# The causal mask of an attention stage put into the score banks by ScalarE copies, where TensorE products with an identity put it before

## The reference, cut to what matters

```python
x = x + _L0_xattn_ref(_layernorm(x, axis=-1), ctx_512, L0_xattn_Wq, L0_xattn_Wkv_expand, L0_xattn_Wout)
...
scores = jnp.einsum('bhqd,bhkd->bhqk', qh, kh) * inv_sqrt_d
causal = jnp.tril(jnp.ones((sq, sk), dtype=bool))
scores = jnp.where(causal, scores, jnp.finfo(scores.dtype).min)
attn = jax.nn.softmax(scores, axis=-1)
out = jnp.einsum('bhqk,bhkd->bhqd', attn, vh)
```

## Time and profile before

| what | value |
|---|---|
| median of 3 runs | 667.65 us (663.9 to 668.47) |
| the profiled execution: its time, its span | 663.85 us, 662.3 us |
| TensorE busy over the span | 593.4 us (90%) |
| VectorE, ScalarE, GpSimd busy | 406.2 us (61%), 294.2 us (44%), 161.9 us (24%) |
| mean granted TensorE clock | 0.957 of full |
| attention stage | 0 to about 143 us of the span |

### The profile page before, as it was taken

The page is one execution under the profiler, slowest core; times in us unless marked ns, Lnnn a source line. Parts: engine busy times, 40 slices in busy tenths (PEclk is TensorE's granted clock), DMA queues, the critical chain, the costliest instruction groups (busy, mean ns, idle before and its releaser), DMA issues.

```text
span 662.3 us, 10646 instructions
## 1 busy us (share of the span) xinstructions
PE 593.4 (90%) x3622; PEld 468.4 (71%) x3642; DVE 406.2 (61%) x790; ACT 294.2 (44%) x477; POOL 161.9 (24%) x245
## 2 busy tenths in 40 slices
PE   4887999765888758699999999999999999999995
PEld 3666877562555436488888888888888888888884
DVE  5766778757999844656766555555555555555553
ACT  3477666433998843534444332333323322333232
POOL 6434495927676744000000000000000000000000
PEclk9899999767999976999999999999999999999999
DMA  9500000020000031445545113111231222241121
GB/s 254 183 2 1 2 2 2 1 64 2 1 1 1 1 127 51 115 108 148 139 118 140 52 68 124 64 64 64 64 127 63 63 63 65 79 109 63 64 63 47
DMA packets 37465, 45.91 MB, mean 69 GB/s; under 512 B 10720, under 2 KB 24688, under 8 KB 37296
## 3 DMA queue, kind: packets, MB, share of 16 engines
q1 hardware_dynamic: 34304, 41.19, 20.8%
q0 software_dynamic: 1008, 3.67, 1.7%
q10 hardware_dynamic: 2112, 0.52, 0.4%
HBM read 41.04 MB, written 4.33 MB: 68 GB/s over the span
## 4 chain that ended last, share of the span: by engine, by line
PE 60%; ACT 1%; POOL 1%; DVE 1%; issue 1%; DVEq 0%; POOLq 0%
PE psY L1341 6%; PE psG L1328 6%; PE psY L1344 6%; PE psY L1343 6%; PE psG L1329 6%; PE psG L1330 6%; PE psU L1328 6%; PE psU L1330 6%; PE psU L1329 6%; PE psAux L1269 1%; PE psT L1269 1%; PE psY L1289 1%; PE psT L1354 1%; POOL r_rstd L1235 1%; ACT gw L1455 0%
## 5 line engine op out<-in xcount | busy, mean ns | idle before, releaser
L1427 ACT ACTIVATE act_hi<-x_tok 128x512 fp32r<-128x512 f32 x88 | 55.7, 633 | 161.9 <-DVE x_tok L1556 161.9
L1549 DVE TENSOR_TENSOR x_tok<-psU,x_tok 128x512 f32<-128x512 f32 x88 | 60.8, 692 | 103.1 <-PE psU L1330 100.6
L1560 DVE TENSOR_TENSOR act_lo<-x_tok,act_hi 128x512 fp32r<-128x512 f32 x88 | 60.8, 692 | 62.6 <-ACT act_hi L1427 62.5
L1421 ACT ACTIVATE x_tok<-psG 128x512 f32<-128x512 f32 x88 | 52.7, 601 | 58.0 <-PE psG L1330 58.0
L1246 POOL DMA_DIRECT2D out_dram<-x_tok x3 | 2.3, 773 | 300.8 <-DVE x_tok L1567 300.8
L1341 PE MATMUL psY<-act_hi,wd_lo 128*128 128x512 f32 x176 | 71.0, 404 | 5.0 <-DVE act_lo L1560 5.0
L1328 PE MATMUL psG<-h3T_hi,wg_lo 128*128 (+1 forms) x176 | 69.9, 397 | 0.3 <-DVE logit L1593 0.3
L1344 PE MATMUL psY<-act_hi,wd_hi 128*128 128x512 f32 x176 | 69.2, 393 | 0.0
L1343 PE MATMUL psY<-act_lo,wd_hi 128*128 128x512 f32 x176 | 69.1, 392 | 0.0
L1329 PE MATMUL psG<-h3T_lo,wg_hi 128*128 (+1 forms) x176 | 69.0, 392 | 0.0
L1330 PE MATMUL psG<-h3T_hi,wg_hi 128*128 (+1 forms) x176 | 69.0, 392 | 0.0
(11 more groups left out here) (223 smaller groups left out, 1160.5 us busy)
## 6 DMA issues: line engine op xcount, KB each, us to landing
cw_rows<-cw_spill SPq DMA_DIRECT2D x80, 128.0 KB, 2.9
cw_rows<-cw_spill SPq DMA_DIRECT2D x16, 224.0 KB, 2.9
cw_rows<-cw_spill SPq DMA_DIRECT2D x16, 192.0 KB, 2.7
w_stage<-in_L_ffn_w_gate_dram SPq DMA_DIRECT2D x11, 256.0 KB, 2.9
w_stage<-in_L_ffn_w_up_dram SPq DMA_DIRECT2D x11, 256.0 KB, 2.8
cw_rows<-cw_spill SPq DMA_DIRECT2D x16, 160.0 KB, 2.5
wg_nat<-in_L_attn_w_gate_dram SPq DMA_DIRECT2D x1, 2048.0 KB, 16.3
x_spill<-x_tok SPq DMA_DIRECT2D x1, 2048.0 KB, 7.3
```

The source lines that it names most:

```text
L1421: nc.scalar.activation(a[s % 2][:, :], psG[s % 2][:, :], ACT.Silu).then_inc(s_silu, 1)
L1427: nc.scalar.activation(a_hi[s % 2][:, :], a[s % 2][:, :], ACT.Copy).then_inc(s_ahi, 1)
L1549: nc.vector.tensor_tensor(a[s % 2][:, :], psU[s % 2][:, :], a[s % 2][:, :], ALU.mult).then_inc(s_t, 1)
L1560: nc.vector.tensor_tensor(a_lo[s % 2][:, :], a[s % 2][:, :], a_hi[s % 2][:, :].bitcast(F32), ALU.subtract).then_inc(s_alo, 1)
```

## The change

ScalarE gets a new step `masked(j, u)`: a copy of the mask from SBUF (bf16) into the score bank u % 2, as soon as VectorE has taken the shifted scores of step u out of it. TensorE's two mask products stay for the very first half (pair 0, half 0) only; the other halves wait for the count of the copies instead (`s_masked`). The wait for `s_sub` stays in place. The last pair needs no copies behind its steps 2 and 3.

```diff
+        s_masked = b.sem("a_masked")
...
+                def masked(j, u):
+
+                    need(act, s_sub, 4 * j + u + 1)
+                    nc.scalar.activation(psS[u % 2][:, :], k.causal[:, :, :].rearrange("p h s -> p (h s)"), ACT.Copy
+                                         ).then_inc(s_masked, 1)
...
                     if two:
                         exps(i - 1, 0)
+                        masked(i - 1, 0)
                     if three:
                         probs_out(i - 2, 2)
                         probs_out(i - 2, 3)
                     if two:
+                        masked(i - 1, 1)
                         exps(i - 1, 1)
...
                         exps(i - 1, 2)
+                        if i < NP:
+                            masked(i - 1, 2)
+                            masked(i - 1, 3)
                         exps(i - 1, 3)
...
-                    for r in range(2):
-                        nc.tensor.matmul(psS[r][:, :], k.identb[:, :],
-                                         k.causal[:, :, :].rearrange("p h s -> p (h s)"), start=True, stop=True,
-                                         skip_group_check=True)
+                    if j == 0 and t == 0:
+                        for r in range(2):
+                            nc.tensor.matmul(psS[r][:, :], k.identb[:, :],
+                                             k.causal[:, :, :].rearrange("p h s -> p (h s)"), start=True, stop=True,
+                                             skip_group_check=True)
+                    need(pe, s_masked, 4 * j + 2 * t)
```

## The result

The changed kernel takes 672.2 us (median of 7 runs, 670.81 to 675.67) against 667.65 (7 runs, 663.9 to 669.64): a ratio of 1.0083, 95% interval 1.005 to 1.0116. It is slower by 0.8%, near the forecast of 671, and inside the 1% that was called hard to tell. Its profiled execution took 673.75 us with a span of 672.2, 9.9 more than the one before. That is twice the difference of the medians, and the last experiment says why.

A forecast was written before the change was run, and what follows sets the result against it. The prediction took a loop over TensorE, VectorE and ScalarE in the attention stage as the bound. Copies and removed products summed to 14c - 8m = 6.72 - 3.52 = +3.2 us on 667.65, forecast 671, range 662 to 680.

The forecast's parts named there:

- The loop: Attention stage: path over TensorE, VectorE and ScalarE said to set the pace, 13.54 us a plain turn.
- plain turns: Attention turns between 4 and 7, without weight sums: said to grow from 13.54 to about 14.06 us.
- The term c: Time of one ScalarE mask copy from SBUF to PSUM: taken as 0.48 us, 0.54 as other end.
- The term m: Time of one pair of TensorE mask products taken away: 0.44 to 0.53 us, taken as 0.44.
- TensorE's reserve: TensorE's 0.34 us wait ahead of attend 2: removing the 7 first-half pairs was said only to lengthen it.
- c - m: Turn 1 to 2: one copy added, one pair of products removed; the copy ahead of exponential 3 hides.
- 3c - m: Turns 2 to 3 and 3 to 4, with weight sums: three copies added, one pair of products removed, each.
- 2c - m: Turns 4 to 5, 5 to 6 and 6 to 7: two copies added, one pair of products removed, each.
- c - 2m: Turn 7 to 8: input scales hide one copy, one stays; the removed pair counts twice at halved clock.
- The wait of attend 2: TensorE's wait for pT ahead of attend 2: from 0.34 to 1.7 us in plain turns, some 1.9 in turn 3.
- The clock rival: Longer TensorE waits ahead of attend 2 drop its clock again and again: 675 to 680 us, chance 0.25.
- one more drop at most: Condition of the main forecast: loop grows, TensorE's clock drops at most once more; 667 to 675 us, chance 0.52.

The follow-up runs named there:

- the last experiment: Kernel before, unedited, profiled and timed once more: ratio 1.002, profiled span 666.3 us against 662.3.
- with the wait filled: Changed kernel with TensorE doing the products of the queries twice in turns 2 to 7: 667.49 us, ratio 1.0029 against the kernel before.
- products gone: Kernel before without TensorE's 30 mask products and with no copies, mask left out behind the first half: 659.26 us, ratio 0.9913.

## Why the prediction was right

**The loop** of the plain turns was read rightly in each step: it runs from the scores over VectorE, ScalarE's last exponential, `pT` copies and `hT_hi`, VectorE again, exponential 0 and `pT` to attend 2. Moving one copy by two places, or dropping two of the four, changed the turn by one step each. Four turn lengths that were on record before their runs, 14.6, 13.10, 14.13 and 13.61, were met within 0.02 us (the 14.13 had been read in the changed kernel's profile). VectorE's wait for `hT_hi` grew from 0.38 to 0.88 us, the 0.5 that was forecast.

**The term c** (0.48, with 0.54 as its other end) was a little low: 0.52 ahead of `pT`, 0.54 ahead of exponential 3. With 0.53 the sum is 14 x 0.53 - 3.52 = +3.9 instead of +3.2. A plain turn was said to be 14.06 and is 14.13. That ScalarE reaches PSUM faster than SBUF, as the Trainium skill has it in "ScalarE: Activation LUTs" ("Step-by-step: what each stage is for"), holds but is small: the copy takes 592 ns on average into the banks and 622 into the spare tile.

**The term m** was taken as 0.44 and is 0.44 (2.67 to 2.23). The 0.09 us ahead of the scores' smaller weights stayed. That first halves lie in TensorE's reserve was shown by the run without the products.

**What was hidden and what was not**: the copies of steps 1 and 2 in plain turns cost nothing, as predicted. Outside the plain turns three terms were off. Second half to second half, with no slow stretch in between except in turn 8, where both kernels have it:

| interval | forecast | measured | from |
|---|---|---|---|
| 1 to 2 | c - m = +0.04 | +0.47 | 13.82 to 14.29, changed kernel |
| 2 to 3 | 3c - m = +1.0 | +1.02 | 15.47 to 16.49, with the wait filled |
| each plain turn | 2c - m = +0.52 | +0.59 | 13.54 to 14.13 |
| 7 to 8 | c - 2m = -0.4 | -1.15 | 15.22 to 14.07, changed kernel |

In turn 1 to 2 the row statistics covered less than half of the copy ahead of exponential 3: `hT_lo` had no wait before, and now waits 0.30 us and starts 0.34 later.

```profile
31.40 0.69 DVE L263 TENSOR_TENSOR hT_lo<-R,hT_hi 128x512 fp32r<-128x512 f32 x1 [0.30 <-ACT hT_hi L480]
```

In turns with weight sums the size is right and its parts are not. The pair of products is not on the loop there (16.41 against 16.42 without it). Of the two copies ahead of exponential 1 one fits into idle time that the forecast did not count:

```profile
51.48 0.63 ACT L499 ACTIVATE prob<-sub 128x512 f32<-128x512 f32 x1 [0.47 <-DVE sub L280]
```

So it is 2c and not 3c - m; with these values the two differ by 0.1 us. In turn 7 the input scales did cover the copy of step 3, but they are also shorter by themselves, 2.28 us (123.98 to 126.26) instead of 2.91 (114.71 to 117.62, where `x_tok` starts in the earlier trace rows). Two of their steps, before and then after:

```profile
115.11 0.69 DVE L172 TENSOR_SCALAR dq_all<-in_top,wmean 128x8 f32<-128x8 f32 x1
...
116.51 1.07 DVE L175 TENSOR_SCALAR rscale_all<-rscale_all 128x8 f32<-128x8 f32 x1
```

```profile
124.38 0.23 DVE L172 TENSOR_SCALAR dq_all<-in_top,wmean 128x8 f32<-128x8 f32 x1
...
125.57 0.65 DVE L175 TENSOR_SCALAR rscale_all<-rscale_all 128x8 f32<-128x8 f32 x1
```

Why was not tested. With the interval 3 to 4 taken like 2 to 3, the measured ones add up to +3.1 us, near the forecast's +3.2; that the ends of the sum cancel is luck.

**The wait of attend 2** was forecast at 1.7 and is 1.79; in turn 3 at 1.9 and is 1.94.

**The clock rival** is real, and the forecast's "one more drop at most" was the wrong count: the changed kernel's profile has three in turns 3 to 6. The price a drop was given, 2.6 us at most, held there: turns 5 to 6 and 6 to 7 took 15.24 and 14.43 around one, 14.14 without, 1.4 us in all, as only the scores and what follows fell into it. By the rival's own sum the time should then have been 675 or more. It still came out near 671, since the kernel before pays too. Its turns 2 to 4 trip the clock in some executions. Its median (667.65) is near the execution that paid (667.81), while the profile that the sum was made against (663.85) had not paid. So the forecast's total is right in part by luck: the clock was left out on both sides. The step that fails is the reading "a wait of 1.43 us left the clock at 2.4 GHz": true of that execution, not of the kernel.

How much of the 0.8% is the loop and how much the clock can be told roughly. Filled waits bring the ratio from 1.0083 to 1.0029. But filling also heals turns that are slow in the kernel before, so the difference, 0.5%, is more than the clock's part in the loss; it is no strict bound, since one slow stretch stayed.

## What to carry to other kernels

- Idle time of an engine is worth something only where work can be put without standing ahead of a result that is waited for. The same copy cost 0.52 us a plain turn ahead of the `pT` copies and nothing behind them. Look for what the engine was waiting for, and put the new work behind the step that follows on it.
- Before moving work off the busiest engine, split it by place. Half of these products lay in that engine's own reserve and were free where they were; only the other half was worth moving.
- One profiled execution is one draw of the clock. Compare the lengths of undisturbed turns, which agree to 0.02 us between executions, and not spans, which here differ by 4 us for the same program.

## What the runs showed of the hardware that was not expected

- Equal waits of TensorE end differently. In the changed kernel a wait of 1.79 us left the scores at 1.09 us, and one of 1.80 in the next turn was followed by scores of 1.99. In the kernel before, waits of 1.62, 1.43 and 1.43 us were followed by full clock in one execution, and waits of 1.62, 1.41 and 1.43 by 1.2 GHz in the next. A longer wait is no surer sign: 2.63 us left the clock up (products gone, turn 8), 0.51 us did not (filled, turn 4). The rule of the Trainium skill in "TensorE: Matmul & The Clock Gate" ("Why this matters for your kernels"), that gaps between bursts send the clock down, agrees with the trace in kind; but here the clock fell behind gaps of 1.4 us, which are shorter than those the page warns of, and in some executions only.
- The same VectorE step on the same 128x8 tile (`dq_all<-in_top,wmean`) took 0.69 us in one program's execution and 0.23 us in another's. No run tests why.
- Repeated products, put into such waits, brought the changed kernel from 0.8% to 0.3% over the kernel before.
